# Sixteen experts ahead of twelve spline products: a new order of turns and PSUM banks

## The reference

```python
# block 1, feed-forward: 16 experts with room for 128 tokens each, top 2 per token
buf = zeros(16, 128, 256).at[e, posc].add(x_pairs)
h = silu(einsum(buf, W1)) * einsum(buf, W3)
out = einsum(h, W2)
y_pairs = out[e, posc] * (w * valid)[:, None]        # each token takes its two rows back
y = y_pairs.reshape(T, 2, D).sum(axis=1) + shared
x = x + attention1(xn) + y
xn = layernorm(x)
# block 2, feed-forward: three 1024 x 256 weights are rebuilt from control points by a cubic spline
gate_w, up_w, down_w = (spline_reconstruct(cp, ...) for cp in (gate_cp, up_cp, down_cp))
inter = silu(xn @ gate_w.T) * (xn @ up_w.T)
x = x + attention2(xn) + inter @ down_w.T
```

## Time and profile before

| | before |
|---|---|
| median of 3 runs | 1214.29 us |
| lowest and highest | 1212.21 and 1215.8 us |
| the profiled execution | 1220.07 us |
| its span, first to last instruction | 1218.5 us |
| its mean granted TensorE clock | 0.951 |
| busy, share of the span | PE 91%, DVE 70%, ACT 53%, POOL 41% |

### The profile page before, as it was taken

How to read it: one execution, slowest core, us unless ns; L and a number is a source line. 1 busy time by engine, 2 the same in 40 slices (tenths; PEclk the granted TensorE clock), 3 DMA queues, 4 the chain that set the end, 5 groups by cost and what they waited for, 6 DMA issues and landing times.

```text
span 1218.5 us, 17434 instructions
## 1 busy us (share of the span) xinstructions
PE 1105.5 (91%) x6542; PEld 724.2 (59%) x6556; DVE 850.5 (70%) x1602; ACT 642.6 (53%) x982; POOL 498.0 (41%) x549
## 2 busy tenths in 40 slices
PE   3699999999999898899679999999789988998998
PEld 2466686755665464675367998988334543553445
DVE  7986866668658898855577335267877779668751
ACT  6555547465569896643145233242187166465473
POOL 5765748365524526312573142243431331161131
PEclk9788999999999999898789999999699999998999
DMA  6715244334350101167370000006814526315420
GB/s 210 237 40 163 64 131 149 97 90 133 77 207 35 36 1 44 60 208 244 96 74 27 1 1 1 1 27 153 206 37 123 140 55 158 104 55 140 107 72 18
DMA packets 86116, 116.42 MB, mean 96 GB/s; under 512 B 29617, under 2 KB 43281, under 8 KB 85265
## 3 DMA queue, kind: packets, MB, share of 16 engines
q1 hardware_dynamic: 47792, 70.28, 19.2%
q0 software_dynamic: 38240, 45.03, 15.1%
HBM read 81.54 MB, written 40.40 MB: 100 GB/s over the span
## 4 chain that ended last, share of the span: by engine, by line
PE 60%; DVE 17%; issue 8%; ACT 8%; DMA 4%; POOL 3%; SPq 0%; DVEq 0%; ACTq 0%; POOLq 0%
PE pair L693 21%; PE bank L693 18%; PE bank L772 6%; PE pair L762 4%; DVE max L1157 4%; PE pair L751 4%; ACT probs L1681 2%; PE pair L712 1%; DMA qs<-kept_max 1%; PE pair L792 1%; POOL gathered L2092 1%; PE bank L780 1%; DVE hidden L1213 1%; DVE hidden L1215 1%; PE pair L962 1%
## 5 line engine op out<-in xcount | busy, mean ns | idle before, releaser
L1157 DVE TENSOR_REDUCE max<-pair 128x2 f32<-128x1024 f32 (+3 forms) x256 | 252.4, 1019 | 57.8 <-PE pair L751 33.3
L1681 ACT ACTIVATE probs<-pair 128x1024 f32<-128x1024 f32 (+3 forms) x256 | 212.5, 864 | 104.3 <-PE pair L762 85.7
L751 PE MATMUL pair<-ks,qs 64*128 64x512 f32 (+3 forms) x512 | 112.1, 458 | 23.9 <-DVE max L1157 11.4
L2013 POOL TENSOR_TENSOR h_low<-hidden,h_high 128x512 fp32r<-128x512 f32 x64 | 83.5, 1310 | 101.0 <-ACT h_high L1719 100.6
L772 PE MATMUL bank<-probs,v 128*32 128x512 f32 (+3 forms) x1024 | 117.8, 546 | 2.7 <-POOL probs L2057 1.3
L762 PE MATMUL pair<-qs,ks 64*128 64x512 f32 (+3 forms) x512 | 103.0, 436 | 10.7 <-DVE max L1157 2.8
L751 PEld LDWEIGHTS pair<-ks,qs 64*128 64x128 f32 x512 | 50.5, 197 | 82.1 <-DVE max L1157 34.4
L762 PEld LDWEIGHTS pair<-qs,ks 64*128 64x128 f32 x512 | 46.6, 190 | 77.5 <-ACT probs L1681 24.5
L1713 ACT ACTIVATE hidden<-pair 128x512 f32<-128x512 f32 x64 | 38.1, 598 | 80.5 <-PE pair L693 65.8
L2110 POOL TENSOR_TENSOR h<-mix_h,h 128x512 bf16<-128x512 f32 x48 | 54.9, 1167 | 61.2 <-DMA h<-comb 35.3
L2057 POOL TENSOR_SCALAR_AFFINE_SELECT probs<-probs 128x256 f32<-128x256 f32 x128 | 50.1, 406 | 72.3 <-ACT probs L1681 71.6
(11 more groups left out here) (330 smaller groups left out, 2686.7 us busy)
## 6 DMA issues: line engine op xcount, KB each, us to landing
kept<-q_high SPq DMA_DIRECT2D x64, 256.0 KB, 4.2
qs<-kept POOLq DMA_DIRECT2D x32, 512.0 KB, 4.2
ks<-kept POOLq DMA_DIRECT2D x32, 512.0 KB, 4.9
kept<-q_low SPq DMA_DIRECT2D x32, 256.0 KB, 4.3
expert_in<-in_experts_in SPq DMA_DIRECT2D x16, 352.0 KB, 4.1
expert_out<-in_experts_out SPq DMA_DIRECT2D x16, 256.0 KB, 5.6
h<-comb SPq DMA_DIRECT2D x4, 1024.0 KB, 5.4
tern_raw<-in_ffn_in SPq DMA_DIRECT2D x8, 256.0 KB, 6.0
```

What stands on the lines that cost most here:

```text
L751: made = mm(to[:, hh, 0:n], m.qs[k][slot][r0:r0 + STACK, p, qt * P:(qt + 1) * P], m.ks[k][slot][r0:r0 + STACK, p, 0:n], start=True, stop=k ...
L1157: V.tensor_reduce(m.max[:, g % 2, :, p, qt], to[:, :, 0:n], AX.X, ALU.max).then_inc(*s.done("top"))
L1681: A.activation(m.probs[(2 * kt + p) % 4][:, :, q0:T], to[:, :, q0:T], ACT.Exp, scale=0.25).then_inc(*s.done("exp"))
L2013: Q.tensor_tensor(m.h_low[k][:, j, :], m.hidden[k][j % 2][:, :], m.h_high[k][:, j, :].bitcast(F32), ALU.subtract).then_inc(*s.done("low"))
```

## The change

Only the two tables change, `DUE` and `TAKEN`: the same instructions, in another order and with other PSUM banks. No step is added or removed. Of 1098 steps on PE 230 change their turn, on DVE 360 of 845, on ACT 360 of 869, on POOL 248 of 428 and on SP 22 of 165, most of them by one to three places. The large moves are around the experts. The numbers of the diff, read as orders:

| engine | before | after |
|---|---|---|
| PE, from `expert_in(10)` on | in 10, out 9, out 8, fold 11, spline (0,2) (0,0), out 11, fold 10, spline (0,1) (1,0) (1,2) (1,1), turn 12, out 10, turn 13, turn 15, in 13, in 12, in 15, fold 13, fold 12, spline (2,0), turn 14, out 13, fold 15, in 14, out 12, fold 14, out 15, out 14, spline (2,1) (3,0), merge 0, merge 1, spline (2,2) (3,1) (3,2), turn(2,0) | out 9, out 8, fold 11, in 10, out 11, fold 10, turn 12, out 10, turn 13, turn 15, in 13, in 12, fold 13, in 15, fold 12, out 13, turn 14, in 14, fold 15, out 12, fold 14, out 15, out 14, spline (0,0) (0,2) (0,1) (1,0) (1,2) (1,1), merge 1, merge 0, spline (2,1) (2,0) (3,0) (2,2) (3,1) (3,2), turn(2,0) |
| DVE | seven sums among the experts, cubic 3, gated and folded 14, sums (2,0) (2,1) (3,0) (2,2) (3,1), combine (0,0), sum (3,2), stat, combine (0,1) to (0,3) with stats, ... | folded 14, six sums, cubic 2, combine (0,0) (0,1), two stats, sums (2,0) (2,1), cubic 3, combine (0,2) (0,3), two stats, four sums, cut_low(2,0), merge_low(0), ... |
| ACT | norm (2,0,*) four in a row | norm (2,0,1) (2,0,2) (2,0,0), spline_high (2,2), norm (2,0,3) |
| POOL | eight spline_low, gather (0,0) (0,1) (1,0) (1,1), root(2,0), gather (2,0) (2,1) (3,1), two spline_low, root(2,1), gather (3,0), two spline_low, low(2,0,1) | spline_low (0,0), gather (0,0), low (0,1), gather (0,1), low (0,2) (1,0) (1,2), gather (1,0), low (1,1) (2,0), root(2,0), low (2,1), gather (1,1) (2,0) (2,1), low (3,2), root(2,1), gather (3,1), low (3,0) (2,2) (3,1), low(2,0,0), low(2,0,1), gather (3,0) |
| SP | spline_load 0 and 1 right behind the load of expert 11, then fetch 12, ...; spline_load 2 ahead of the load of expert 14, spline_load 3 behind the store of 11 | fetch 13, spline_load 1, fetch 12, spline_load 0, fetch 15, store 6, loads of 13 and 12, ...; spline_load 2 and 3 behind all stores |
| POOL, block 3 | `based(3, 2)` and `with_xn(2)` behind `cast3`, ahead of `root(3, 3)`; `based(3, 3)` and `with_xn(3)` ahead of and behind `max_bring(3, 2, 2)`; `mix_comb(2, 11)`, `bring(3, 3, 0)`, `max_bring(3, 2, 3)`, `bring(3, 3, 1)` | the first two around `low(2, 3, 7)`, ahead of `bring(3, 0, 0)`; the others around `max_bring(3, 0, 3)` and `bring(3, 1, 1)`; `bring(3, 3, 0)`, `bring(3, 3, 1)`, `mix_comb(2, 11)`, `max_bring(3, 2, 3)` |

(In the row of POOL "low (0,1)" with two numbers is short for `spline_low(0, 1)`.)

The core of the diff:

```diff
-    "merge": "577 578",
-    "expert_turn": "497 496 499 502 518 516 525 522 537 533 541 539 557 559 567 560",
-    "expert_in": "500 501 508 505 520 519 529 524 540 538 545 542 562 561 570 563",
-    "expert_fold": "504 506 515 509 528 521 532 527 543 544 552 548 565 564 572 569",
-    "expert_out": "511 510 517 512 531 523 534 530 547 546 558 551 571 568 574 573",
-    "spline": "550 553 549 554 556 555 566 575 579 576 580 581",
+    "merge": "575 574",
+    "expert_turn": "498 497 499 502 518 516 525 522 537 533 539 540 551 553 561 554",
+    "expert_in": "500 501 508 505 520 519 528 524 541 538 548 543 556 555 562 558",
+    "expert_fold": "504 506 515 509 529 521 532 527 544 542 550 547 559 557 565 563",
+    "expert_out": "511 510 517 512 531 523 534 530 546 545 552 549 564 560 567 566",
+    "spline": "568 570 569 571 573 572 577 576 579 578 580 581",
...
-    "combine": "437 440 441 444 446 449 450 455 457 458 465 466 486 476 468 490",
-    "cubic": "411 414 422 429",
-    "spline_sum": "415 418 416 419 421 420 432 433 435 434 436 438",
-    "merge_low": "448 447",
...
+    "combine": "431 432 438 439 449 448 452 453 465 459 463 464 487 490 471 486",
+    "cubic": "422 413 430 437",
+    "spline_sum": "424 426 425 427 428 429 435 436 443 442 444 445",
+    "merge_low": "447 457",
...
-    "spline_high": "471 474 473 484 481 478 490 492 502 504 494 495",
...
+    "spline_high": "485 487 486 488 490 489 493 492 497 500 501 502",
...
-    "root": "2 17 40 57 102 169 237 257 287 293 296 304 315 326 333 347",
-    "based": "5 55 54 74 317 329 345 402",
-    "with_xn": "319 331 346 405",
...
+    "root": "2 17 40 56 102 170 235 257 285 291 302 307 315 321 330 347",
+    "based": "5 54 60 66 317 332 340 365",
+    "with_xn": "319 335 342 369",
...
-    "gather": "283 284 285 286 288 289 294 290",
-    "spline_low": "275 276 278 280 279 277 281 282 292 295 291 297",
...
+    "gather": "276 278 282 287 288 289 298 292",
+    "spline_low": "275 277 279 280 283 281 284 286 294 293 295 290",
...
-    "expert_load": "65 61 64 62 76 74 79 78 88 83 90 91 101 100 106 104",
-    "fetch": "67 66 68 69 70 73 71 72 80 82 84 87 94 97 99 98",
-    "store_y": "77 75 85 81 95 86 96 89 102 103 107 108 112 111 114 113",
-    "spline_load": "92 93 105 109",
+    "expert_load": "65 61 64 62 76 74 79 78 88 83 90 92 100 99 105 104",
+    "fetch": "67 66 68 69 70 73 71 72 80 82 84 87 95 93 102 97",
+    "store_y": "77 75 85 81 91 86 98 89 101 103 106 107 110 109 112 111",
+    "spline_load": "96 94 113 114",
...
-    "expert_turn": "6777777777776667",
-    "expert_in": "4220242002244222",
-    "expert_fold": "7767666776766766",
+    "expert_turn": "6777777777766667",
+    "expert_in": "4240424204440204",
+    "expert_fold": "7767766676766766",
...
-    "qk2": "0444",
...
+    "qk2": "4442",
```

More of the change, by code:

```diff
@@ L321 @@
 TAKEN = {name: [int(bank) for bank in banks] for name, banks in {
-    "tern_sum": "202020224044",
-    "turn": "4204020222402044",
-    "qk": "4024202222024242",
-    "vals": "2042224440004240",
-    "score": "4424000204044040200022440240222420044404024240044242004400404442402020444224200000040044024420024442200004400020204020220044424004020422022244442440444240424040422420200424400402024004020042002404020400024242222044024424040244222404044224242004402240442020",
-    "prob": "4220022002440444202044222202024020422004024204420022200204404224242422420224022040024202020224240442040442040202224240200242404022424402240224022200224220440224042022420040244044240040222442400204224000402022042022220204024004022004240442004424024402400024",
@@ L328 @@
-    "weigh": "66666666666677776666777777777777777766666666777766666666666666667777666666666666777766666666666677776666777777777777666677776666",
-    "back": "67666776776777767776777776667676",
-    "rows": "442004040424",
-    "out": "76667767777676767676677667667776",
-    "unit": "2402022420004202400242044002244240422040400240204200044220242044",
-    "down": "77776677",
-    "mean": "7667",
-    "proj": "0044020402200440",
-    "gate": "6667667776676776",
+    "tern_sum": "200220224044",
+    "turn": "4224024222020044",
@@ new lines @@
+    "qk": "4024202200024242",
+    "vals": "2004224442004240",
+    "score": "4424000204004040200022440240222420044404024240044242004400404442402024044424200040044224024420024442200004400020204020220044424004020422022244442440444240424040422402200424400402022044020002002404020400024242222044024424040240222404044224242004402240442020",
+    "prob": "4224022002440440242044222202024020422004024204420022200204204224202022200424022040024202020224240442040442040202224240200242044022424402240224022200224240420242042040420040244044244440222442400204224000402022042022220204024004022004240442004424024402400024",
@@ L337 @@
+    "weigh": "77776666666677776666777766667777777777777777777766666666666666666666777766666666666677776666666677776666777777777777666666666666",
+    "back": "77666776666677777776677776677776",
+    "rows": "242004000422",
+    "out": "76767767777676767676676776666767",
+    "unit": "2402022420004204400242044002444222422040040240200044020440042244",
+    "down": "77776777",
+    "mean": "6667",
+    "proj": "0044020200220440",
+    "gate": "6667667777676776",
     "gamma": "4024",
-    "inflow_turn": "2202",
+    "inflow_turn": "0202",
@@ L339 @@
     "mem_turn": "77776666",
-    "shared": "0202440220420402",
+    "shared": "0202440220420442",
     "count": "7666",
```

8 lines of the change are left out of this document (4 added, 4 removed), and 208 rows, old and new, of the table DUE.

## The result

The change made the kernel slower: 1247.83 us (1243.72 to 1248.52, three runs) against 1214.29, a ratio of 1.0258 with a 95% interval of 1.0221 to 1.0296. I had said 1208.8 and a range of 1202.5 to 1217.0. The profiled execution of the changed kernel took 1247.83 us, its span 1246.3, so 27.8 more than the profiled one of before; that one lay 5.8 us above its median, which is why the traces differ by less than the medians.

The account below looks back on a forecast made before the run. The prediction took PE as the bound, idle ahead of qk2(0) behind POOL and DVE, and full from 660. Gains of 4.8 to qk2(0) and 0.7 behind it made 5.5 us: 1214.29 to 1208.8 us, range 1202.5 to 1217.

Parts of the forecast that it names:

- Experts without splines: On PE, the experts no longer wait for seven spline products: 4.0 us wait for weights, experts end 7.9 us sooner.
- the 13.5: PE's expert work from the wait at expert_turn(12) to the last expert product, put at 13.5 us.
- the high end: Upper case for the experts' gain on PE, 9.6 us instead of 7.9, with that stretch at full clock.
- First gather and `root(2, 0)`: On POOL: first gather at 580.0, gain 8.7 us; root(2, 0) at 603.2 instead of 609.09, gain 5.9 us.
- The 3 us that I gave DVE in hand: DVE was to finish its sums, combines and statistics at about 599 to 600, 3 us ahead of root(2, 0).
- my 22.5 us of work in one piece: DVE's work from 576: eight spline sums, two cubics, four combines and four statistics, summed to 22.5 us.
- From `root` to `qk2(0)`: From root(2, 0) on POOL to qk2(0) on PE: 8.0 us before; qk2(0) forecast at 612.3, gain 4.8 us.
- 0 to 1.5, I take 0.5: Delay ahead of turn(2, 0) from the last splines sharing banks and waiting for sums: 0.5 us taken.
- the gain of 4.8: qk2(0) on PE was to start at 612.3 instead of 617.12, 4.8 us sooner.
- Behind `qk2(0)`: From qk2(0) to 660: earlier low(2, 0, *) against combines waiting for later gathers; between +3 and -2, gain 0.7 us taken.
- The rest of the deal: Neighbour exchanges in stages 0, 1 and 3 and block 3's moves on POOL: 0 in all, from -2 to +2 us.
- The splines become the path: Rival, chance 0.12: products, sums and merges between experts and turn(2, 0) bind, PE at half clock; 4 us slower, 1218.3.

Follow-up runs that it names:

- e5b: Before with only the expert region in changed order, repaired so turn(2, 0) and qk2(0) pass the last spline products; 1224.42 us, ratio 1.0032 to before.
- e9: e5b with qk2_low(0), weight2(0, 2) and gated(2, 0, 1) moved ahead of combines on DVE; 1223.65 us, ratio 1.0052 to before.
- e12: e9 with merge_low(1) on DVE moved right behind the spline sum (3, 2); 1225.77 us, ratio 1.0063 to before.

## Why the prediction was wrong

**Experts without splines: right.** The wait for `expert_out(12)`'s weights (3.46 us for 4.0) and the end of the experts (-7.5 for -7.9) came as summed; the clock held up (0.91 and 0.79 in the two stretches from 560 to 600, against 0.83 and 0.83 before). In before only 2.9 us of the 13.5 were at half clock and not 3.5 (granted 0.72 in 568 to 572, 1.00 behind), which touches the high end alone.

**First gather and `root(2, 0)`: near.** 581.2 and 604.1 for 580.0 and 603.2. The 3 us that I gave DVE in hand were gone: its sums waited for PE between (3.36, 0.39, 1.70 and 1.54 us), which my 22.5 us of work in one piece left out, and its last statistic but one took 2.18 us beside two subtractions of POOL, for 0.17 before. So DVE released `root`, but only 0.18 us after POOL was through with these subtractions; POOL's 22.9 us from the first gather (23.2 summed) set the date just as much.

**From `root` to `qk2(0)`: the first failed step.** "0 to 1.5, I take 0.5" for the last splines in front of `turn(2, 0)` was 6.9 us more than that: 16.0 for 9.1. The products, their sums and the turn are one chain of two engines that wait for each other, two rounds long, at half clock. I had costed the waits singly. e5b shows it: past them, `turn(2, 0)` is 6.0 us sooner. Against the date of `qk2(0)` in before this made a loss of 3.0 us out of the gain of 4.8.

**Behind `qk2(0)`: wrong in kind.** A gain of 0.7 was a loss of 3.1. Up to 2.6 us of it go with the clock, which I had costed only ahead of `qk2(0)`: the profiled execution had 0.88 granted in 633 to 674, before 0.94 in 617 to 655, that is 9.8 and 4.6 us at half speed. And e5b, e9 and e12 show that a gain would not have gone through. The fully busy rows from 660 on the earlier trace rows said that PE is the bound from there, not that the end of the units at 655 hangs on PE.

**"The rest of the deal": the largest error.** 0 (from -2 to +2) was 21.6 us: block 0 5.5, the front of block 1 7.6, behind block 2's first units 8.5. Of the moves I "followed those that move far" and priced each by what it leaves, `based(3, 2)` and `with_xn(2)` at 0 to 0.4 of gain, where the new place of `with_xn(2)` cost 3.3. `max_bring(3, 2, 3)` was the one that I saw ("2 us later, beside a transfer that lands no sooner"); its own transfer became the last to land. The exchanges of neighbours I took as free, and 5.1 us of block 0 come from them, on ACT and POOL. In the front of block 1 they come to 7.6, of which up to 3.3 go with the clock and the rest stays open.

**The rivals.** "The splines become the path" named the right chain, but made it hang on clock lost among the experts, which did not come. Its own sum takes 1.5 us for merges and splines, where the sentence ahead of it says 4; with 4 it would have been 1220.8. None held a loss outside the experts, so nothing in the range reached 1247.

## What to carry to other kernels

A table of turns that is dealt anew has to be priced over its whole length: here four fifths of the loss lay away from the move that I had studied. Cutting the two orders at places where they have done the same steps, one region at a time and one engine at a time, found where it was. A difference of 2 or 3 us between two single traces is not yet a finding, though: look at the granted clock of the same stretch, and at other traces with the same orders. For a step that moves, look at what it will run beside and who is queued behind it at the new place, not only at what it leaves. A gain on the way to a busy stretch is real only if the end of that stretch moves with it; follow it to a step whose date is known on both sides.

## What was not expected of the hardware

The same 2.3 us of idle PE left the clock at full in one trace and at half in two, which made 2.8 and 3.0 us of difference in eight products. One 128x1024 multiplication on DVE took 3.31 us instead of 1.23 beside one addition of the same shape on POOL.
